# The second norm's root a half step later, its rows on ScalarE, its transposes a half step further

## The reference

```python
h = layernorm(x)                                            # first norm
red = segment_sum(h[src] + relvectors[edge_type], dst)      # messages summed per node
x = x + gru_cell(red, h, w_ih, w_hh, b_ih, b_hh)            # gates r, z, n
n = layernorm(x)                                            # second norm: (x - m) / sqrt(v + eps)
top2 = top_k(n @ Wg + bg, 2)                                # two of 8 experts, each with weight 1
x = x + sum over top2 of (gelu(n @ W1[e] + b1[e]) @ W2[e] + b2[e])
```

## Time and profile before

| | |
|---|---|
| median of the runs | 1530.57 us |
| the profiled execution's own time | 1530.21 us |
| its span in the profile | 1527.8 us |
| TensorE (PE) busy | 1273.4 us, 83% |
| VectorE (DVE) busy | 997.3 us, 65% |
| GpSimd (POOL) busy | 990.3 us, 65% |
| ScalarE (ACT) busy | 715.0 us, 47% |

### The profile page before, as it was taken

One profiled execution on the slowest core, in us unless ns is written; L12 is line 12 of the kernel. 1 busy time (PEld: TensorE's weight loads), 2 busy tenths in 40 slices (PEclk: granted clock), 3 DMA queues, 4 the chain that ended last, 5 costly groups with the idle time before them and its releaser, 6 DMA issues. The chain is left out here.

```text
span 1527.8 us, 35906 instructions
## 1 busy us (share of the span) xinstructions
PE 1273.4 (83%) x12781; PEld 1042.6 (68%) x12781; DVE 997.3 (65%) x2766; ACT 715.0 (47%) x1465; POOL 990.3 (65%) x868
## 2 busy tenths in 40 slices
PE   1168998999899899988988888796754899999995
PEld 1145676777677677667776776676653799999994
DVE  7866775667676667887787777677355455555552
ACT  6524454545544444444443333333121667667763
POOL 2077775677767677777777777777743255555554
PEclk8559999999999999999999989898876899999998
DMA  9586633444445444445445444344483455555552
GB/s 294 176 206 196 194 97 94 139 138 139 128 125 144 111 129 135 141 138 144 143 140 147 138 128 119 117 114 121 121 237 117 102 94 84 95 91 93 88 93 25
DMA packets 131972, 201.47 MB, mean 132 GB/s; under 512 B 28358, under 2 KB 99551, under 8 KB 130643
## 3 DMA queue, kind: packets, MB, share of 16 engines
q0 software_dynamic: 60032, 110.76, 30.5%
q1 hardware_dynamic: 71763, 88.35, 19.8%
HBM read 152.08 MB, written 51.10 MB: 133 GB/s over the span
## 5 line engine op out<-in xcount | busy, mean ns | idle before, releaser
L709 POOL DMA_INDIRECT ring<-h_table,idx x648 | 672.9, 1038 | 283.0 <-issue 203.1
L1722 PE MATMUL P<-hs,amat 128*126 128x512 f16 (+2 forms) x1470 | 384.1, 393 | 0.0
L827 ACT ACTIVATE amat<-P 128x300 f16<-128x300 f32 (+2 forms) x436 | 184.0, 470 | 236.9 <-PE P L1709 234.5
L763 POOL DMA_INDIRECT out_dram<-yo,xrows x112 | 177.2, 1583 | 161.5 <-DVE yo L1586 105.6
L1722 PEld LDWEIGHTS P<-hs,amat 128*126 128x126 f16 (+2 forms) x1470 | 174.0, 133 | 81.1 <-issue 6.8
L1704 PE MATMUL P<-cone,lone 128*128 128x294 f16 (+5 forms) x920 | 181.0, 297 | 40.3 <-ACT amat L827 32.8
L718 POOL DMA_INDIRECT expert_rows<-xrow,slots x100 | 130.8, 1308 | 69.0 <-DVE slots L1329 39.8
L1577 DVE SCALAR_TENSOR_TENSOR gl<-gT,scales,gh 128x512 f16<-128x512 f32 x112 | 84.9, 758 | 138.8 <-ACT gh L954 138.8
L1186 DVE TENSOR_TENSOR cone<-src_t,twice 128x1176 f16<-128x1176 f16 (+5 forms) x230 | 165.8, 721 | 0.0
L1936 PE MATMUL P<-xh,w_all 128*128 128x256 f16 x896 | 157.4, 274 | 0.0
L1949 PE MATMUL P<-w_all,gh 128*128 x896 | 149.8, 273 | 0.6 <-DVE gl L1577 0.6
(11 more groups left out here) (244 smaller groups left out, 2677.4 us busy)
## 6 DMA issues: line engine op xcount, KB each, us to landing
raw<-in_L_ffn_W_dram SPq DMA_DIRECT2D x32, 512.0 KB
xrows<-expert_rows SPq DMA_DIRECT2D x56, 257.0 KB, 3.1
ring<-h_table,idx POOLq DMA_INDIRECT x648
w_parts<-parts SPq DMA_DIRECT2D x16, 512.0 KB, 6.7
w_all<-w_parts SPq DMA_DIRECT2D x8, 1024.0 KB, 15.5
h_in<-h_table SPq DMA_DIRECT2D x25, 250.0 KB
x<-in_x_dram SPq DMA_DIRECT2D x25, 250.0 KB
out_dram<-x SPq DMA_DIRECT2D x25, 250.0 KB
```

Of the source, the lines that this page charges most:

```text
L709: nc.gpsimd.indirect_dma_start(out=ring[:, r, j, :], out_offset=None, in_=h_dram, in_offset=bass.IndirectOffsetOnAxis(ap=idx[:, slot, g * ...
L763: nc.gpsimd.indirect_dma_start(out=out, out_offset=bass.IndirectOffsetOnAxis(ap=xrows[:, b % XR, j, D:D + 1].bitcast(I32), axis=0), in_=yo ...
L827: nc.scalar.activation(amat[:, b % 2, :, s * aw:(s + 1) * aw], bank[:, 0:HIS * aw].rearrange("p (h w) -> p h w", w=aw), ACT.Copy).then_inc ...
L1722: nc.tensor.matmul(both, amat[:, b % 2, hi, 0:used], hs[:, hi, :], start=(hi == 0), stop=False)
```

## The change

- On SyncE the first load of `raw` for the conversion, with its wait for the sixteenth maximum, stands ahead of the loop instead of in its turn 1.
- On ScalarE `root` stands at b+8 instead of b+7, behind the next tile's `bias_hn`. A new `norm_rows`, behind the bank copies of b+8, makes both halves of `xrow` from x with a bias and a scale per row. `high_x2` stands at b+9 instead of b+8.
- On VectorE `second_norm` no longer makes the rows. It makes their bias (mean times the reciprocal, negative) and signals `coef_ready`.
- On TensorE `transpose_x2` stands at b+9 instead of b+8.
- `low_x2`, `score`, `choose`, `rank` and `number` keep their half steps.

```diff
...
@@ -647,14 +647,13 @@
                 if job:
                     sp.wait_ge(w_maxed, job)
                 load_raw(job)
+            sp.wait_ge(w_maxed, WJOBS)
+            load_raw(0)
             for i in range(TILES):
                 if i + 1 < TILES:
                     sp.wait_ge(h_trans, i + 1)
                     sp.dma_start(h_in[:, :, :], node_rows(h_dram, i + 1)).then_inc(h_loaded, 16)
                 job = i - 1
-                if job == 0:
-                    sp.wait_ge(w_maxed, WJOBS)
-                    load_raw(0)
                 if i == FREE_TILE:
                     sp.wait_ge(head_free, 1)
                     sp.wait_ge(w_stored, 16 * WJOBS)
@@ -873,6 +872,13 @@
                 act.wait_ge(var_ready, i + 1)
                 nc.scalar.activation(std[0:SUB, 0, 0:2], var[0:SUB, 0, 0:2], ACT.Sqrt, scale=DOWN * DOWN).then_inc(std_ready, 1)
 
+            def norm_rows(i):
+                act.wait_ge(coef_ready, i + 1)
+                for j in range(2):
+                    ins = nc.scalar.activation(xrow[:, i % 2, j, 0:D], x1[:, j, :], ACT.Identity,
+                                               bias=nmr[0:SUB, 0, j:j + 1], scale=rstd[0:SUB, 0, j:j + 1])
+                ins.then_inc(x2n_ready, 1)
+
             def high_x2(i):
                 act.wait_ge(x2_trans, i + 1)
                 nc.scalar.activation(x2h[:, :, :].rearrange("p k t -> p (k t)"), P[5][:, 0:KT * T], ACT.Copy).then_inc(x2h_ready, 1)
@@ -892,7 +898,7 @@
                     n, s = divmod(h, 2)
                     for i in stage_of(h, 2):
                         bias_hn(i)
-                    for i in stage_of(h, 7):
+                    for i in stage_of(h, 8):
                         root(i)
                     if h + 4 in ADDED_AT:
                         high_sums(ADDED_AT.index(h + 4))
@@ -911,6 +917,8 @@
                     for g in groups_of(h)[len(bursts[0]):] if bursts else []:
                         move_group(g)
                     for i in stage_of(h, 8):
+                        norm_rows(i)
+                    for i in stage_of(h, 9):
                         high_x2(i)
                     if s == 1 and n + 1 < NS:
                         move_counts(n + 1)
@@ -1290,10 +1299,8 @@
                     dve.wait_ge(scattered[i % 2], 64 * (i // 2))
                 link(nc.vector.reciprocal(rstd[0:SUB, 0, 0:2], std[0:SUB, 0, 0:2]))
                 nc.vector.tensor_scalar(xrow[:, i % 2, :, D:D + 1].bitcast(I32), tok[0:SUB, :].unsqueeze(2), float(T * t), None, ALU.add)
-                for j in range(2):
-                    ins = nc.vector.tensor_scalar(xrow[:, i % 2, j, 0:D], x1[:, j, :], mv[0:SUB, 0, j, 0:1], rstd[0:SUB, 0, j:j + 1],
-                                                  ALU.subtract, ALU.mult)
-                ins.then_inc(x2n_ready, 1)
+                nc.vector.scalar_tensor_tensor(nmr[0:SUB, 0, 0:2], mv[0:SUB, 0, 0:2, 0], -1.0, rstd[0:SUB, 0, 0:2],
+                                               ALU.mult, ALU.mult).then_inc(coef_ready, 1)
 
             def low_x2(i):
                 dve.wait_ge(x2h_ready, i + 1)
@@ -1853,7 +1860,7 @@
                             head_burst(bursts[m + 1])
                     for i in stage_of(h, 1):
                         gate_hn(i)
-                    for i in stage_of(h, 8):
+                    for i in stage_of(h, 9):
                         transpose_x2(i)
                     for i in stage_of(h, 11):
                         rank(i)
```

More of the change, by code:

```diff
@@ L493, in gnn_ffn_kernel @@
             h_loaded x_loaded x_stored h_trans hT_ready h_l_ready red_ready hn_done hn_ready r_done r_ready rhn_ready
-            z_done z_ready in_done pre_n n_ready gru_ready gru_trans x1_ready var_ready std_ready x2n_ready x2_trans
+            z_done z_ready in_done pre_n n_ready gru_ready gru_trans x1_ready var_ready std_ready coef_ready x2n_ready x2_trans
             x2h_ready x2l_ready scores_done mask_ready ranks_done slots_ready
@@ L507, in gnn_ffn_kernel @@
          h_loaded, x_loaded, x_stored, h_trans, hT_ready, h_l_ready, red_ready, hn_done, hn_ready, r_done, r_ready, rhn_ready,
-         z_done, z_ready, in_done, pre_n, n_ready, gru_ready, gru_trans, x1_ready, var_ready, std_ready, x2n_ready, x2_trans,
+         z_done, z_ready, in_done, pre_n, n_ready, gru_ready, gru_trans, x1_ready, var_ready, std_ready, coef_ready, x2n_ready, x2_trans,
          x2h_ready, x2l_ready, scores_done, mask_ready, ranks_done, slots_ready,
```

## The result

The changed kernel takes 1566.55 us (median of four runs, 1558.26 to 1576.12), the kernel before beside it 1530.36 (four, 1526.72 to 1532.8). The ratio is 1.0249, with a 95% interval of 1.0219 to 1.0278: 36 us slower. The forecast was 1560.

What follows compares the result with a forecast made beforehand. TensorE was taken to bound the loop before 600 us and the expert layers, GpSimd the loop from 600 to 1050 us. Terms -6 + 2 + 18 + 8 + 3 + 5 = +30 gave 1560 us, range 1540 to 1584.

Steps and rivals of the forecast that it cites:

- The raw weights: Near 240 us: issuing the load before the loop removes ScalarE's 4.27 us wait and some low-clock time, -6 us.
- Root and rows at zero: On ScalarE, bank copies come later in one half step and earlier in another; taken as 0, range -5 to +6 us.
- The first half: 200 to 600 us: VectorE's late low part makes TensorE wait for the numbering, 18 us in tiles 2 to 7, 2 in tile 0.
- these six tiles take 14.7 us longer: Tiles 2 to 7: VectorE's 77.61 us from low part to numbering against TensorE's 67.15, plus 0.7 us a tile.
- Tiles 9 to 14: Second half: 24.0 us by the same count, less 11.9 of TensorE's waits for gathers; 8 us taken, bounds 0 and 16.
- The first rival: After 600 us GpSimd hides the second half altogether; +14 us, 1544, chance 0.17.
- The clock: Some ten new waits for the numbering lower TensorE's clock while today's short waits vanish; 3 us, bounds 0 and 12.
- The last tiles: Tile 22's rows, expert weights and last x come later, and transposes stand behind gates; 5 us, bounds 2 and 9.
- The sum: Whole kernel: all terms together +30 us on the profiled 1530.2, forecast 1560; this case's chance 0.56.
- Serial everywhere: Whole loop: nothing hides the waits and each brings a clock dip; +52 us, 1582, chance 0.12.
- A drain at each switch of tables: On ScalarE: a table switch costs a drain besides the load, and bank copies wait for it; +8, 1568, chance 0.04.

Runs made afterwards that it cites:

- the change with filled waits: The changed kernel with 16 unused matmuls ahead of TensorE's wait for the numbering in tiles 10 to 15; 1563.67 us, ratio 1.0240 to the kernel before.

## Why the prediction was right, and where it was not

**The raw weights.** -6 was forecast, 7 measured (3.8 to 10.2 after the interval times 1530). In the changed kernel TensorE still waits 2.38 us there.

**Root and rows at zero.** Right for the change as a whole: the late transposes alone cost as much as all of it. It is not a property of the rows, which cost 12 to 14 us when the transposes do not move.

**The first half.** The size was right, the way to it mostly wrong, and that the parts came to the size was luck. Forecast were 20 us of waiting without the clock; 18 to 21 were measured, by the two splits above. But the step "these six tiles take 14.7 us longer", by VectorE's work against TensorE's, rested on the numbering alone, and TensorE's waits for it rose only from 4.7 to 10.3 us, not to 3 to 5 a tile. Each wait that TensorE has earlier in the tile moves it back, and the numbering is then less late. The scores took 5.3 us. The waits for the bank copies rose from 14.7 to 23.3: the prediction listed "the builds, the choice, the blend and the numbering" behind the low part and left the addition out, which has ScalarE's tanh and the copies behind it. It had put the copies at an even zero, for the root's sake.

**Tiles 9 to 14.** 8 were forecast, 11 measured over the second and third stage. But TensorE is idle only 2 to 4 us longer there and busy 8 longer, so what grew was not the forecast's term, the net waiting. That TensorE's own waits for rows go first was right (18.6 us to none). The first rival, that GpSimd hides this half, is out.

**The clock.** This is the term that was mis-sized most: 3 forecast, 10 to 17 measured in the first stage alone, by the split that is taken. Its row was also read too generously: of the 6.8 us at the low clock, 3.1 lay inside the wait of 6.24 us, which ended at 246.24, and not after it. The short waits of before did not vanish as was assumed; new ones were added to them. In the second stage of the changed kernel TensorE's waits for one tile read like this:

```profile
723.59 0.69 PE L1817 MATMUL P<-mask,tri 125*125 125x8 f16 x5 [2.37 <-DVE mask L1327]
727.22 1.19 PE L1792 MATMUL P<-ident,oT 128*125 128x128 f32 x4 [1.75 <-DVE slots L1336]
```

The stretch around them, columns as for the stages (the granted clock is the third from the end):

```profile
723.40:733.60 10.20, 8.01 (x76) 6.02 (x77) 9.51 (x25) 1.54 (x4) 7.68 (x7) 0.50 0.27 75
```

Between sums 11 and 60 the clock stood at 0.50, the 1.2 GHz level, in nine stretches with the early load and in 17 with the late transposes. The Trainium skill (TensorE: Matmul & The Clock Gate, HAM oscillation — how this bites in real kernels) tells of a kernel that waits for data at every step and falls back to the slow clock each time; this trace agrees in kind, with those 17 stretches.

**The last tiles.** 5 forecast, 6.1 measured in the changed kernel's profiled execution (3.6 with the late transposes alone).

**The sum.** The profiled execution of the early load took 1520.21 us, 10 less than that of the kernel before (1530.21). From there the stages give -10 + 31 + 10.5 + 3.6 = +35 for the late transposes (1565.40). For the changed kernel's profiled execution they give -10 + 34.8 + 11 + 6.1 = +42; its first stage also starts at 216.12 us instead of 212.20, which makes it +46 (1576.12). The medians give +36. So the forecast of +30 was low by the clock of the first stage, and 3 us short in the second half. The last gather ends at 1158.9 us instead of 1119.8, 39 us later in this execution and 32 with the late transposes alone, where 20 were forecast.

**The rivals.** Serial everywhere (1582) was right in its reason, a dip with each wait, and overshot in the second half (16 against 11) and in the last tiles (9 against 3.6 to 6.1). A drain at each switch of tables would show as idle time at the loads; they have 0.4 us before each 25 of them, and what stands behind starts at once (in the changed kernel a load from 512.45 to 513.73 us, the root at 513.75). So the 1.38 us which the Trainium skill (ScalarE: Activation LUTs, What ACT_TABLE_LOAD costs) gives for it is not seen here.

## What to carry to other kernels

When an operation is moved later, list everything that stands behind its consumer on that engine, and follow each item to the engines that wait for it: here the costliest single one was a 0.67-us addition, two engines away from the wait that it caused. A stage number is not a time: within the same half step the place ahead of the gates or behind them decided over nearly the whole loss. And price a wait of a nearly full TensorE at more than its length, by what the clock does in the rows behind the waits of the kernel at hand; where another engine sets the pace, as GpSimd seems to do after the first stage here, that price may not be paid.

## What was not expected of the hardware

TensorE's idle time in the first stage, length less busy time, is 46.3, 46.5 and 46.3 us with the late transposes alone, in the changed kernel and in the change with filled waits. The last two run the same program up to there, and the first differs only in root and rows. Yet the stage took 393.92, 397.68 and 389.30 us at clocks of 0.95, 0.94 and 0.96. Without length times (1 - clock) all three have 374 us, and the spread of 8.4 us is all in TensorE's busy time (347.64, 351.23 and 342.96). So the same waits cost 15 to 24 us of clock from one execution to the next.

That does not carry over to whole executions. In the 105 executions of the experiments' kernels, each set against the mean of its own kernel, the time is longer by only 0.1 us for each microsecond more of time x (1 - granted clock), and the correlation is 0.2. Part of the low clock lies where TensorE has little to do, as in the last tiles of the early load (0.65, with TensorE busy for 30.27 of 70.47 us), so the product is not a time lost.
